# Four routing steps and one softplus pass taken off VectorE in a one-core attention, scan and mixture-of-experts tower

## The reference

```python
h = tok(x)                         # windows of 8x8 tokens, 8 heads of 8, rotary positions, softmax attention
h = h + mamba(layernorm(h))        # RMS norm, conv of 4 taps, silu, then:
#   delta = softplus(x_branch @ projDelta_w.T + b);  dA = exp(delta * -exp(A_log))
#   h_t = dA_t * h_(t-1) + (x_branch * delta)_t * B_t          128 channels x 16 states, 4096 steps per image
#   y = (sum over states of h_t * C_t + x_branch * D) * silu(z);  out = y @ out_proj_w.T + residual
h = h + ffn(layernorm(h))          # 6 experts of 3 layers; router:
#   p = softmax(relu(f @ rw1 + b1) @ rw2 + b2);  top 2 of p;  weights = softmax of these two
#   combined = sum over the two of weight * expert_out
```

## Time and profile before

| | |
|---|---|
| median of 3 executions | 1615.11 us |
| profiled execution | 1619.14 us |
| its span | 1617.4 us |
| VectorE busy | 1276.6 us (79%) |
| TensorE busy | 1217.3 us (75%) |
| GpSimd busy | 1095.3 us (68%) |
| ScalarE busy | 1033.0 us (64%) |
| mean granted TensorE clock | 0.842 of 2.4 GHz |

### The profile page before, as it was taken

One profiled execution on the slowest core, in us unless ns is written; L12 is line 12 of the kernel. 1 busy time (PEld: TensorE's weight loads), 2 busy tenths in 40 slices (PEclk: granted clock), 3 DMA queues, 4 the chain that ended last, 5 costly groups with the idle time before them and its releaser, 6 DMA issues. The chain is left out here.

```text
span 1617.4 us, 25667 instructions
## 1 busy us (share of the span) xinstructions
PE 1217.3 (75%) x7972; PEld 553.4 (34%) x7972; DVE 1276.6 (79%) x1389; ACT 1033.0 (64%) x1973; POOL 1095.3 (68%) x1475
## 2 busy tenths in 40 slices
PE   3674868796978777787879787877878696767565
PEld 1441425252524334252525243342515252212121
DVE  1112798888989898898989898989989898889841
ACT  2335757678585858686776858585867767473521
POOL 2014697768777777778787777777787877776630
PEclk9977969899898989798988989897979887686755
DMA  2002797786877778677767787786877777878710
GB/s 72 7 9 81 211 251 207 202 219 193 228 184 234 200 215 212 206 220 208 218 198 219 193 230 197 219 215 201 224 207 213 203 217 209 228 209 245 216 36 7
DMA packets 205983, 301.63 MB, mean 186 GB/s; under 512 B 70220, under 2 KB 70424, under 8 KB 205720
## 3 DMA queue, kind: packets, MB, share of 16 engines
q1 hardware_dynamic: 205848, 299.99, 65.9%
HBM read 274.75 MB, written 20.97 MB: 183 GB/s over the span
## 5 line engine op out<-in xcount | busy, mean ns | idle before, releaser
L1281 POOL TENSOR_TENSOR hc<-hs,c_rep 128x512 f32<-128x512 f32 x512 | 655.7, 1283 | 246.5 <-DVE hs L1053 246.3
L1053 DVE TENSOR_TENSOR_SCAN hs<-bank,state,xd 128x512 f32<-128x512 f32 x512 | 644.4, 1271 | 35.0 <-issue 23.5
L789 ACT ACTIVATE bank<-dl,a_neg 128x512 f32<-128x512 f32 x512 | 350.7, 688 | 259.1 <-DVE hs L1053 257.1
L1043 DVE TENSOR_TENSOR xd<-xd,bank 128x1024 f32<-128x1024 f32 x256 | 305.6, 1194 | 11.1 <-PE bank L434 8.3
L449 PE MATMUL bank<-hc,wts 128*32 128x512 f32 x1024 | 173.0, 740 | 2.9 <-POOL hc L1281 1.6
L557 PEld LDWEIGHTS both<-q_diag,k_heads 128*128 128x128 f32 x1024 | 153.5, 215 | 10.6 <-issue 5.0
L557 PE MATMUL both<-q_diag,k_heads 128*128 128x128 f32 x1024 | 152.5, 298 | 0.0
L545 PE MATMUL both<-k_heads,q_diag 64*64 64x512 f32 x512 | 85.3, 738 | 69.7 <-DVE neg_max L1074 42.8
L1074 DVE TENSOR_REDUCE neg_max<-both 128x16 f32<-128x1024 f32 x64 | 77.1, 1205 | 61.6 <-PE both L545 61.6
L714 PE MATMUL bank<-e,wts 64*64 64x512 f32 x384 | 67.5, 777 | 68.8 <-ACT e L977 68.8
L682 PE MATMUL bank<-wT,w_sel 128*128 128x512 f32 x96 | 67.7, 705 | 52.4 <-DVE ew L1142 36.2
(11 more groups left out here) (169 smaller groups left out, 2138.8 us busy)
## 6 DMA issues: line engine op xcount, KB each, us to landing
xd<-xdel_rows SPq DMA_DIRECT2D x512, 256.0 KB, 4.3
dl<-delta_rows SPq DMA_DIRECT2D x512, 256.0 KB, 4.0
delta_rows<-delta SPq DMA_DIRECT2D x16, 512.0 KB, 3.5
xdel_rows<-xdel SPq DMA_DIRECT2D x16, 512.0 KB, 3.0
xin<-in_x_dram SPq DMA_DIRECT2D x32, 128.0 KB, 3.4
q_diag<-rot SPq DMA_DIRECT2D x64, 64.0 KB, 2.8
out_dram<-res SPq DMA_DIRECT2D x256, 16.0 KB
wts<-in_packed_dram SPq DMA_DIRECT2D x1, 1528.5 KB, 6.5
```

The source lines that it names most:

```text
L789: act.activation(decay_ps[n % 2][:, :], dl[:, n % 4, :], ACT.Exp, scale=a_neg[:, g:g + 1])\
L1043: dve.tensor_tensor(pair, pair, b_ps[:, :].unsqueeze(1).to_broadcast([128, 2, BAND]), ALU.mult)\
L1053: dve.tensor_tensor_scan(hs[:, n % 4, :], decay_ps[n % 2][:, :], xd[:, n % 8, :], state[:, g:g + 1], ALU.mult, ALU.add).then_inc(scanned.s ...
L1281: pool.tensor_tensor(hc[:, n % 8, :], hs[:, n % 4, :], c_rep[:, BAND * h:BAND * h + BAND], ALU.mult)\
```

## The change

Softplus: VectorE's pass over 1024 elements (L1120) goes. ScalarE computes 1 + e into `ln_d` in the place of the log, subtracts 1 of it into `xdel` one slot later, and takes the log of `ln_d` in place in slot 15: four passes instead of two. Routing: the maximum is reduced into PSUM (`top_ps`, in a bank of the attention) and is_equal reads it there; the step st13 = (st17 - 1) * st12 becomes two GpSimd steps; 1 + st14 and the copy of the first float32r part go to GpSimd. TensorE's scores of a chunk also wait until is_equal has read `top_ps`.

```diff
         top_ps = both[:, 0, 0:NW]                                  (new)
@@ pe, scores
                 if w == 0:
+                    if has(k - 4):
+                        pe.wait_ge(route_dve.sem, route_dve.at(k - 4, 4))
@@ act, soften
                     act.activation(ex_d[:, :], ex_d[:, :], ACT.Exp, scale=-1.0).then_inc(soft_act.sem, 1)
                     act.wait_ge(soft_act.sem, soft_act.at(k, 1))
-                    act.activation(ln_d[:, :], ex_d[:, :], ACT.Ln, bias=1.0).then_inc(soft_act.sem, 1)
+                    act.activation(ln_d[:, :], ex_d[:, :], ACT.Identity, bias=1.0).then_inc(soft_act.sem, 1)
+                if n == 14:
+                    act.wait_ge(soft_act.sem, soft_act.at(k, 2))
+                    if past(k - 1):
+                        act.wait_ge(kept.sem, kept.at(k - 1, 32))
+                    act.activation(xdel[:, :], ln_d[:, :], ACT.Identity, bias=-1.0).then_inc(soft_act.sem, 1)
+                if n == 15:
+                    act.wait_ge(soft_act.sem, soft_act.at(k, 3))
+                    act.activation(ln_d[:, :], ln_d[:, :], ACT.Ln).then_inc(soft_act.sem, 1)
@@ dve, prepare
-                    dve.tensor_scalar(xdel[:, :], ex_d[:, :], 1.0, -1.0, ALU.add, ALU.add).then_inc(soft_dve.sem, 1)
@@ dve, route
-                    dve.tensor_reduce(st[:, 16, :], rt[:, 4, :, :], X_AXIS, ALU.max).then_inc(done.sem, 1)
+                    dve.tensor_reduce(top_ps, rt[:, 4, :, :], X_AXIS, ALU.max).then_inc(done.sem, 1)
...
-                    dve.tensor_tensor(rt[:, 5, :, :], rt[:, 4, :, :], wide_of(16), ALU.is_equal).then_inc(done.sem, 1)
+                    dve.tensor_tensor(rt[:, 5, :, :], rt[:, 4, :, :], top_ps.unsqueeze(2).to_broadcast([128, NW, E]),
+                                      ALU.is_equal).then_inc(done.sem, 1)
...
-                    dve.scalar_tensor_tensor(out=st[:, 13, :], in0=st[:, 17, :], scalar=-1.0, in1=st[:, 12, :],
-                                             op0=ALU.add, op1=ALU.mult).then_inc(done.sem, 1)
...
-                    dve.tensor_scalar(st[:, 15, :], st[:, 14, :], 1.0, None, ALU.add).then_inc(done.sem, 1)
-                    dve.wait_ge(route_pool.sem, route_pool.at(k, 6))
+                    dve.wait_ge(route_pool.sem, route_pool.at(k, 9))
                     dve.tensor_reduce(st[:, 18, :], rt[:, 9, :, :], X_AXIS, ALU.max).then_inc(done.sem, 1)
...
-                    dve.tensor_copy(w_parts[:, :, 0, :], rt[:, 13, :, :]).then_inc(done.sem, 1)
@@ pool, prepare
-                        pool.wait_ge(soft_dve.sem, soft_dve.at(k, 1))
+                        pool.wait_ge(soft_act.sem, soft_act.at(k, 3))
@@ pool, route
                     step(8, 7, wide_of(17), ALU.subtract).then_inc(done.sem, 1)
+                    pool.tensor_tensor(st_f[:, 8, :], st_f[:, 17, :], const(6), ALU.subtract).then_inc(done.sem, 1)
+                    pool.wait_ge(done.sem, done.at(k, 6))
+                    pool.tensor_tensor(st_f[:, 13, :], st_f[:, 8, :], st_f[:, 12, :], ALU.mult).then_inc(done.sem, 1)
...
                     step(9, 13, rev, ALU.mult).then_inc(done.sem, 1)
+                    pool.tensor_tensor(st_f[:, 15, :], st_f[:, 14, :], const(6), ALU.add).then_inc(done.sem, 1)
...
+                    pool.wait_ge(done.sem, done.at(k, 12))
+                    pool.tensor_copy(w_parts[:, :, 0, :], rt[:, 13, :, :]).then_inc(done.sem, 1)
```

More of the change, by code:

```diff
@@ L136, in tower @@
         psum += [ctx.enter_context(nc.psum_tensor(f"bank{i}", [128, 512], F32)) for i in range(6, 8)]
+        top_ps = both[:, 0, 0:NW]
         decay_ps, b_ps, y_ps = psum[0:2], psum[2], psum[3]
@@ L165, in tower @@
         w_sel = sb("w_sel", [128, 2 * EP, 128], F32R)
-        eps = sb("eps", [128, 6])
+        eps = sb("eps", [128, 7])
         conv_w = sb("conv_w", [128, 2, 128])
@@ L261, in tower @@
         silu_ready = sig("silu_ready", 1)
-        soft_act = sig("soft_act", 2)
-        soft_dve = sig("soft_dve", 1)
+        soft_act = sig("soft_act", 4)
         soft_pool = sig("soft_pool", 8)
@@ L281, in tower @@
         ln2_pool = sig("ln2_pool", 7)
-        route_dve = sig("route_dve", 12)
-        route_pool = sig("route_pool", 10)
+        route_dve = sig("route_dve", 9)
+        route_pool = sig("route_pool", 14)
         route_act = sig("route_act", 4)
@@ L654, in experts @@
                     fill(use, k)
-                    pe.wait_ge(route_pool.sem, route_pool.at(k, 10))
+                    pe.wait_ge(route_pool.sem, route_pool.at(k, 14))
                     for i in range(4):
@@ L771, in _ @@
             pe.wait_ge(setup_dve, 13)
-            pe.wait_ge(setup_pool, 15)
+            pe.wait_ge(setup_pool, 16)
             pe.wait_ge(setup_act, 3)
@@ L965, in route @@
                     act.activation(rt[:, 13, :, :], rt[:, 8, :, :], ACT.Relu, scale=1e38, bias=1.0).then_inc(route_act.sem, 1)
-                    act.wait_ge(route_dve.sem, route_dve.at(k, 7))
+                    act.wait_ge(route_pool.sem, route_pool.at(k, 7))
                     act.activation(st_f[:, 14, :], st_f[:, 13, :], ACT.Exp).then_inc(route_act.sem, 1)
@@ L1027, in _ @@
             act.wait_ge(placed, 192)
-            act.wait_ge(setup_pool, 15)
+            act.wait_ge(setup_pool, 16)
             act.wait_ge(setup_dve, 13)
@@ L1166, in route @@
                     dve.wait_ge(route_pool.sem, route_pool.at(k, 2))
-                    dve.tensor_reduce(st[:, 16, :], rt[:, 4, :, :], X_AXIS, ALU.max).then_inc(done.sem, 1)
+                    if has(k + 4):
+                        dve.wait_ge(A["v0"].drained, A["v0"].empty(k + 4))
+                    dve.tensor_reduce(top_ps, rt[:, 4, :, :], X_AXIS, ALU.max).then_inc(done.sem, 1)
                     dve.tensor_reduce(st[:, 11, :], rt[:, 2, :, :], X_AXIS, ALU.add).then_inc(done.sem, 1)
                     dve.wait_ge(done.sem, done.at(k, 2))
-                    dve.tensor_tensor(rt[:, 5, :, :], rt[:, 4, :, :], wide_of(16), ALU.is_equal).then_inc(done.sem, 1)
+                    dve.tensor_tensor(rt[:, 5, :, :], rt[:, 4, :, :], top_ps.unsqueeze(2).to_broadcast([128, NW, E]),
+                                      ALU.is_equal).then_inc(done.sem, 1)
                     dve.wait_ge(done.sem, done.at(k, 3))
@@ L1209, in body @@
                         experts(c - 2, odd, SLOTS + n)
-                    if has(c + 1):
-                        prepare(c + 1, n)
                     if has(k):
@@ L1244, in _ @@
             dve.wait_ge(setup_dve, 13)
-            dve.wait_ge(setup_pool, 15)
+            dve.wait_ge(setup_pool, 16)
             rounds(body)
@@ L1422, in _ @@
             pool.memset(state[:, :], 0.0).then_inc(setup_pool, 1)
-            for i, v in enumerate((LN_EPS, RMS_EPS, -0.5 * LN_EPS, -0.5 * RMS_EPS, 1.0 / C, 1.5)):
+            for i, v in enumerate((LN_EPS, RMS_EPS, -0.5 * LN_EPS, -0.5 * RMS_EPS, 1.0 / C, 1.5, 1.0)):
                 pool.memset(eps[:, i:i + 1], v).then_inc(setup_pool, 1)
-            pool.wait_ge(setup_pool, 15)
+            pool.wait_ge(setup_pool, 16)
             pool.wait_ge(setup_dve, 13)
```

23 lines of the change are left out of this document (6 added, 17 removed).

## The result

The changed kernel takes 1631.09 us (median of 14, 1622.95 to 1639.95), the kernel before 1615.87 us in the same sessions (14 runs, 1614.22 to 1623.25). The ratio is 1.009, with a 95% interval of 1.0077 to 1.0104: the change makes the kernel 0.9% slower. The prediction had 1612 us and a range up to 1624. The profiled execution has a span of 1628.1 us, 10.7 more than before. The medians differ by 15.2: what follows is read from one execution of each kernel and accounts for some 11 of it.

The account below looks back on a forecast made before the run. ScalarE and TensorE bound each round up to the maxima, VectorE behind them. -14 x 0.55 + 2.4 = -5.3 us gave 1610 on the median's scale, the clock's effect 1615; the middle, 1612, was taken, range 1592 to 1624.

Parts of the forecast that it names:

- The division of the round: ScalarE and TensorE lead up to the maxima, VectorE behind them; what is taken from VectorE counts only there.
- the first lock of is_equal: Before the maxima, L1170 takes 1.02 us against its twin's 0.19; removing this was judged worth 0.
- The local sum: Maxima 1.28 us late, VectorE saves 2.20 behind them, `cen` shifts 1.46 against 2.01: 0.55 us gained a round.
- B: Rival: ScalarE's passes hidden better, or clock's return covers part of delay; up to 1.2 us a round gained, 1601; chance 0.09.
- The new wait at the norm's sum: VectorE's L1112 must wait for ScalarE's square, since `cen` comes 1.46 us later; gain 0.55 a round, not 0.92.
- rival C: Slower through GpSimd's late `cen` at L1112: shift up to 3.05 us, each of 14 rounds 1.04 longer, 1632; chance 0.17.
- a rule on two inputs in SBUF: VectorE instructions with two SBUF inputs exclude GpSimd's SBUF reads; some 2.7 us a round would be lock.
- What the clock does to it: Two half-clock stretches on the path give back half of lateness or earliness each; rounds settle where they were, 1615 us.
- rival A: A half-clock stretch shortens as TensorE's gaps before 848 shrink: -14 us, 1598, at most 1568; chance 0.18.
- The one-time costs: ScalarE's two passes ahead of the first chunk's heads +1.94 us, the round after about +0.5.
- the prediction's price: ScalarE's pass over 1024 elements takes 0.97 us; the two passes cost 1.94 if nothing is covered.

Follow-up runs that it names:

- e4: Kernel before plus a useless VectorE reduction of 160 elements in slot 21 of every middle round: 1618.06 us, ratio 1.0007.
- e1: Kernel before with softplus's part of the change alone (ScalarE's four passes, L1120 dropped), routing as before: 1627.08 us, ratio 1.0068.
- e2: Kernel before with routing's part of the change alone, softplus as before: 1613.27 us, ratio 0.9976.
- e6: e2 plus useless TensorE matmuls in slots 4, 9, 11 and 12: 1598.54 us, ratio 0.9883 to the kernel before.
- e7: Kernel before plus useless TensorE matmuls in slots 4, 9, 11 and 12: 1613.94 us, ratio 0.998.
- e8: e6 plus useless matmuls in slots 16 and 22 to 24: 1576.19 us, ratio 0.9754 to the kernel before.
- e10: Kernel before with the useless matmuls of e8, no part of the change: 1597.4 us, ratio 0.9894.
- e12: e8 with more useless matmuls in slots 22 to 25 (17 for 9): 1576.12 us, ratio 0.9762 to the kernel before.
- e15: Kernel before with softplus's part of the change alone and the useless matmuls of e12: 1625.23 us, ratio 1.005.
- e13: Whole change with the useless matmuls of e12: 1601.48 us, ratio 0.9903 to the kernel before.
- e14: Kernel before with the useless matmuls of e12, no part of the change: 1584.41 us, ratio 0.9804.
- e3: Changed kernel plus a useless VectorE reduction of 1024 elements in slot 21 of middle rounds: 1625.19 us, ratio 1.0039 to the kernel before.
- e5: Changed kernel plus useless TensorE matmuls in slots 4, 9, 11 and 12: 1622.93 us, ratio 1.0036 to the kernel before.

## Why the prediction was wrong

**The division of the round was right.** VectorE waits longer for ScalarE ahead of the maxima, as worked out: ScalarE's router step is 1.44 later (1.28 predicted). L1120, L1177 and the first lock of is_equal brought nothing there; the waits of 2.77 and 1.29 took them up.

**The local sum came out right, in part by luck.** Slots 16 to 21 are 0.55 shorter, 0.55 had been predicted. Two of its terms were off and cancelled: the maxima come only 0.59 later and not 1.28, which fits the reason that the prediction gave under B (part of the delay falls before the clock's return), and L1186 lost 0.87 to GpSimd, which its twin before had not. The new wait at the norm's sum did not appear in steady rounds, since `cen` is 0.84 later and not 1.46; rival C, which placed the loss there, was near in its time (1632) and wrong in its place. The prediction also counted L1181 and the cast as locked by a rule on two inputs in SBUF, though each has one. By the trace both are held up all the same: L1181 takes 0.71 with 0.68 left of the GpSimd step beside it and 1.08 with 1.05 left, the cast 1.27 with 1.23 left and 0.16 in a late round with none.

**The step that failed is "What the clock does to it".** It took the two half-clock stretches of a round as given and asked only how much work falls into them: by it the 11 equal rounds would bring 0.8 us together, without it 0.55 each. Rounds 1 to 12 cost 4.3. The step also said that each fall follows a time in which TensorE stood nearly idle; that holds for the first (0.00 busy in 822 to 824), while ahead of the second TensorE was busy for 0.60 us in 844 to 846 and for 1.08 in 846 to 848, and ahead of the fall at 530.5 it was busy from 528.0 on.

The kernel before ran in step with the clock: e4 shows that 0.24 us put on the path of a round leave it at 88.75, and e1, which costs 1.5 us in slots 16 to 21 at full clock, leaves most rounds there too. For a lengthening that part of the step holds. For a shortening it does not. In the changed kernel and in e2, which get through their edited slots earlier, a third half-clock stretch stands at slots 5 to 8 or 11 to 14 in nearly every round.

At the first place TensorE runs matmuls of 18 and 64 columns, ahead of the second it has waits of 1.1 to 1.7 us. In the changed kernel a stretch costs 1.4 to 1.6 us in a round, 2.6 where both stand in it (round 2), and 3.9 where the later one is 10.2 us long (round 6). Over rounds 2 to 11 that is 1.59 us a round, against 0.55 and 0.72 gained. The prediction knew the earliness (rival A hoped for a shorter stretch, and got 3.4 us of one) and never looked at where else the clock might fall.

e2 shows it without softplus's part: it gains 1.84 a round in slots 16 to 21 and 26 to 29 and stands at 88.75 because slots 11 and 14 take 1.6 back; e6 puts matmuls there, and it is 15 us faster than e2, 11 more than the kernel before does by the same matmuls (e7). That the loss of step is what brings the third stretch is argued from these rounds. It is not the whole rule: with the matmuls of e8 in it the kernel before has such a stretch in five of its twelve middle rounds too (e10).

**The one-time costs were too small.** 1.94 + 0.5 had been set; 1.35 + 3.7 were measured. In round 0 slots 16 and 17 are longer by 2.1 in the changed kernel and in e1 alike: the two passes, 1.94 by the prediction's price, show in full there, where it had 0.5. Slot 7 is longer by 1.4, with a half-clock stretch that the kernel before does not have there. Round 13, counted as a gain of 0.55, costs 2.4: slot 7 takes 1.6 of it by a third stretch, and slots 23 and 24 take 2.4, of which slots 16 to 21 give 1.5 back.

**With the clock held, the change does not pay either.** At full clock (e12 to e15) it costs 0.5 us a round in slots 16 to 21. Before, VectorE waited only 0.52 for the scores there; after the change it waits 1.11. e13 is 17 us slower than e14 in the median. In the profiled executions it is 12.7: 2.7 before the first scan, 5.3 in round 0, 5.1 in rounds 1 to 12, 1.0 in round 13, and 1.4 back at the end. So holding the clock did not take the loss away. In the changed kernel as it ran the third stretch took the gain of its rounds; ScalarE's two passes, in the rounds and at the beginning, are the part that stays when the clock is held. How the 15 us of the medians divide between the two is open.

## What to carry to other kernels

When a loop's rounds are all equally long to a hundredth, ask whether they keep step with TensorE's clock: then a part of the path can be lengthened at little cost (0.24 us a round in e4), and shortening it may bring a new half-clock stretch and no time. Hold the clock first, with useless matmuls in TensorE's waits, and judge changes on that kernel. Moving work off the busiest engine pays only where that engine ends the wait, and the engine that takes it must not be the one that others wait for at that place.

## What the runs showed of the hardware

- Rounds of 88.73 to 88.75 us came in six kernels with different work in slots 16 to 21 (before, e1 to e5), and rounds of 85.29 to 85.34 in e8.
- TensorE's clock fell to 1.2 GHz at about 530.5 while TensorE was busy throughout 528.0 to 530.5; in that time it had run matmuls of 18 and 64 columns.
- A VectorE step of 48 elements with two inputs in SBUF takes 0.19 to 0.21 us alone. Beside a long GpSimd step on SBUF it lasts until that one ends: 0.66 with 0.59 left of it, 1.02 with 0.96, 1.29 with 1.23 (L1170 of the kernel before). With one input in PSUM it took 0.20 in 16 of 16 (L1174).
- A copy of 48 elements to float32r took 0.23 us on GpSimd. On VectorE it took 1.20 to 1.27 in the 14 rounds in which GpSimd was in a long step, and 0.16 and 0.19 in the two others.
